# Cross attention on Trainium2: on ScalarE the next unit's exponential ahead of this unit's high half

## The chip, the cores and the metric

The kernel runs on one core of one Trainium2 chip. The metric is the device time of one execution in microseconds (us). Before the change it is 1541.23 us, the median of 3 runs (1541.2 to 1542.07).

## The reference, cut to what matters

The kernel computes a two layer decoder for 8 sequences of 256 tokens with 256 channels: window attention, cross attention, experts, a gated recurrence, a second cross attention and a feed forward part, each with a residual and a layer norm. The change touches only the two cross attentions. What one of them computes (the first masks with an integer mask, the second adds a mask; both have 16 heads of 16 channels and 77 context rows a batch):

```python
Q = proj(query, Wq, bq)
K = proj(key, Wk, bk)
V = proj(value, Wv, bv)
scores = jnp.einsum('bhqd,bhkd->bhqk', Q, K) / np.sqrt(D_K)
scores = jnp.where(m == 0, NEG, scores)
attn = jax.nn.softmax(scores, axis=-1)
x = jnp.einsum('bhqk,bhkd->bhqd', attn, V)
x = x.transpose(0, 2, 1, 3).reshape(b, -1, D_MODEL)
return x @ Wo.T + bo
```

## The kernel before

The stages run one after the other, with a barrier of all engines between them. A cross attention (function `cross_attention`, called twice, tags ca0 and ca1) goes through 8 batches; a batch has 8 units (`UNITS`), numbered c = 0 to 7. A unit is one tile of 128 tokens with 4 of the 16 heads. Each engine runs a queue of its own in the order in which its program is written, and the queues meet only at semaphores. What one unit needs, in the order of the data:

- TensorE `score(b, c)` (L1134): scores of 4 heads, 128 x 308, into one of two PSUM banks.
- VectorE `mask_scores` (L1008 in the second stage, L1010 in the first): masks the scores into `z`. Then `take_maximum` (L1016) writes the maxima of `z` into `top`.
- GpSimd `subtract` (L887): `z` minus the maxima, semaphore `shift`.
- ScalarE `power` (L951): the exponential of `z` into `probs`, semaphore `exped`. Called exp(c) below.
- TensorE `turn_probs` (L1143): transposes the four heads of `probs` into PSUM, semaphore `probs_t`. Called turn(c).
- ScalarE (L959): the high half of the turned probabilities as fp16 into `pth`, semaphore `probs_high`. Called pth(c). It frees nothing by itself: the PSUM bank stays in use until the low half is taken.
- VectorE `probs_rest` (L1021): the low half into `ptl`, semaphore `probs_low`. Called ptl(c). It needs pth(c).
- TensorE `weigh` (L1157): 12 small products of the two halves with the two halves of the values.

`z`, `top`, `probs`, `pth`, `ptl` and the PSUM banks all exist twice, so unit c and unit c + 2 share one.

The loops are staggered by hand. In the pass for unit c:

- TensorE: turn(c), score(c + 2), one step of the projections, weigh(c - 1).
- VectorE: mask(c + 2), ptl(c), top(c + 2), then whatever the unit has besides (normalising, residual and its statistics, the layer norm's last step, values).
- GpSimd: subtract(c + 2), then in some units the masked keys (L881), a token sum (L895) or the root of the variance (L155).
- ScalarE: pth(c), exp(c + 1), then the eviction of the projection step, if it is ScalarE's.

The projection steps come from a planner, the ring `CA`, one a unit: keys (evicted at L937 into `kb`), values, heads (L939, `ot`), mix, tokens (L929, `xt`), query (L932, `q`), heads, mix. They serve the next batch for keys, values, tokens and query, and the one before for the first heads and mix. The first and the last batch leave some out. DMAs are issued from SyncE only: the context and the tokens of the batch after next.

Of the kernel before, what the change touches and what calls it, by code (L numbers as in the profile page):

```python
# [162 lines left out]
def first(b):  # L163

    return isinstance(b, int) and b == 0
# [547 lines left out]
UNITS = TPB * CH // UH  # L713
# [39 lines left out]
def cross_attention(nc, weights, ctx_dram, ident, half, X, next_loads=None):  # L753
    tag, additive = weights.tag, weights.additive
    w, bias, rows, mask = weights.w, weights.bias, weights.rows, weights.mask
    with ExitStack() as ctx:
# [59 lines left out]
        def wait_read(engine, steps, b):  # L816
            CA.wait_read(engine, free, steps, b)
# [6 lines left out]
        def both(batch):  # L824

            def run(engine):
                batch(0, 0, before=False)
                with engine.Fori(0, BATCH // 2 - 1) as i:
                    batch(2 * i + 1, 1)
                    batch(2 * i + 2, 0)  # L830
                batch(BATCH - 1, 1, after=False)
            return run
# [4 lines left out]
        @block.sync  # L837
        def _(sp):
            def load_context(b, par):
                sp.dma_start(context[par][:], ctx_dram[:, :, bass.ds(b * CTX, CTX)]).then_inc(context_loaded[par], 16)  # L840

            def stage(b, par):

                sp.dma_start(xs[par][:], X[:, bass.ds(b * TPB, TPB)]).then_inc(staged[par], 16)

            for b in (0, 1):
                load_context(b, b)
                stage(b, b)
            if next_loads:
                next_loads(sp)  # L850

            def replace(b, par):

                wait_full(sp, "value", 0, b)
                load_context(b + 2, par)
                wait_full(sp, "tokens", 0, b)
                sp.wait_ge(token_sum, (b + 1) * TPB)
                stage(b + 2, par)

            replace(0, 0)  # L860
            replace(1, 1)
            with sp.Fori(1, BATCH // 2 - 1) as i:
                replace(2 * i, 0)
                replace(2 * i + 1, 1)
# [54 lines left out]
        @block.scalar  # L919
        def _(act):  # L920
            act.wait_ge(weights.loaded, 64)

            def step(b, par, kind, i, bank, uses):
                src = shared[bank]
                if kind in ("mix", "value"):
                    return
                act.wait_ge(full[bank], uses + 1)
                if kind == "tokens":
                    ins = act.activation(xt[par][:], src[:].rearrange("p (g q) -> p g q", g=KT_), ACT.Copy)  # L929
                elif kind == "query":  # L930
                    for g in range(KT_):
                        ins = act.activation(q[par][:, g], src[:, g * SEQ:(g + 1) * SEQ], ACT.Identity, bias=bias[:, 0, g:g + 1])  # L932
                elif kind == "key":
                    if not first(b):
                        act.wait_ge(key_masked, b * KT_)
                    for g in range(KT_):
                        ins = act.activation(kb[:, g], src[:, g * CTX:(g + 1) * CTX], ACT.Identity, bias=bias[:, 1, g:g + 1])  # L937
                elif kind == "heads":
                    ins = act.activation(ot[:, i], src[:, 0:DIM].rearrange("p (g q) -> p g q", g=KT_), ACT.Copy)  # L939
                ins.then_inc(free[bank], 1)  # L940

            def value_high(b, par):
                wait_read(act, [("value", 0)], b)
                act.activation(vh[par][0:CTX, :, 0:CD], v[0:CTX], ACT.Copy, scale=SCALE).then_inc(v_high, 1)

            def power(b, c):
                k = c % 2
                act.wait_ge(shift, b * UNITS + c + 1)
                if not (first(b) and c < 2):
                    act.wait_ge(probs_t, b * UNITS + c - 1)  # L950
                act.activation(probs[k][:], z[k][:], ACT.Exp, scale=1.0 if additive else CD ** -0.5).then_inc(exped, 1)  # L951

            def batch(b, par, before=True, after=True):
                for c in range(UNITS):
                    k = c % 2
                    act.wait_ge(probs_t, b * UNITS + c + 1)
                    if not (first(b) and c < 2):
                        act.wait_ge(weighted, b * UNITS + c - 1)
                    act.activation(pth[k][0:CTX], t_bank[k][0:CTX], ACT.Copy, scale=PSCALE).then_inc(probs_high, 1)  # L959
                    if c < UNITS - 1:  # L960
                        power(b, c + 1)
                    elif after:
                        power(b + 1, 0)
                    for kind, i, bank, uses in CA.slot(c, b):
                        d = CA.serves(kind, i)
                        step(b + d, (par + d) % 2, kind, i, bank, uses)
                    if c == 2 and after:
                        value_high(b + 1, 1 - par)

            act.wait_ge(ones, 1)  # L970
            for kind, i, bank, uses in CA.prologue():
                step(0, 0, kind, i, bank, uses)
            value_high(0, 0)
            power(0, 0)
            both(batch)(act)
            for kind, i, bank, uses in CA.epilogue():
                step(BATCH - 1, 1, kind, i, bank, uses)
# [1664 lines left out]
```

## Time and profile before

| | before |
|---|---|
| median of 3 runs | 1541.23 us |
| profiled execution | 1540.88 us, its span 1539.1 us |
| TensorE busy | 1201.4 us (78%) |
| VectorE busy | 1101.3 us (72%) |
| ScalarE busy | 672.9 us (44%) |
| GpSimd busy | 506.7 us (33%) |
| high half of turned probabilities (L959) | 128 instructions, 593 ns each |
| exponentials of the cross attentions (L951) | 128 instructions, 455 ns each |
| low half (L1021) | 128 instructions, 677 ns each |

The first cross attention lies at about 547 to 720 us of the span, the second at about 1271 to 1442. Busy time counts the execution of instructions; an engine that waits for a semaphore is idle, and the profile names what ended the wait. Consecutive instructions of one engine overlap a little, so distances from start to start say more of the pace than durations do. The granted clock is a share of TensorE's full 2.4 GHz: 1.00 is that, 0.50 is 1.2 GHz, values between are a mean over a stretch.

### The profile page before, as it was taken

Reading aid. Unit: us, or ns where it says so; the run is one execution under the profiler, and the core shown is the slowest. Engines: PE = TensorE matmul, PEld = TensorE weight load, DVE = VectorE, ACT = ScalarE, POOL = GpSimd, SP = SyncE. Lnnn points to the kernel's source line nnn. Section 1 sums busy time; section 2 is a strip of 40 time slices with the busy share of each in tenths; the row PEclk is TensorE's granted clock in tenths of the full one; section 3 lists DMA queues with packets and bytes.
Section 4 is the critical chain, followed back from the end, with each engine's and each line's share of the span. In section 5 each row is a group of like instructions: output and inputs, shape, how many; then the busy total and the mean of one; then the engine's idle time right before and its main releaser. Section 6 shows DMA issues by size and latency. Waiting matters only on the chain. (4 is left out here: it accounts for less than half of the span.)

```text
span 1539.1 us, 29853 instructions
## 1 busy us (share of the span) xinstructions
PE 1201.4 (78%) x10299; PEld 988.2 (64%) x10300; DVE 1101.3 (72%) x2315; ACT 672.9 (44%) x1379; POOL 506.7 (33%) x494
## 2 busy tenths in 40 slices
PE   4889888898898869996113566749989957999687
PEld 1577776776777857775113566748878846777576
DVE  5687877777787638886872766646888764888678
ACT  3454544443454325653101333424655523655184
POOL 3212111021110025553723332133453433555323
PEclk8899999998999979997556787969999977999699
DMA  5000000010000000002512332030000002000011
GB/s 187 8 1 9 9 1 10 6 54 3 1 1 1 2 20 20 18 16 86 194 59 95 126 129 86 26 110 17 21 20 10 5 0 79 28 18 7 28 35 48
DMA packets 31079, 61.39 MB, mean 40 GB/s; under 512 B 7610, under 2 KB 20602, under 8 KB 27898
## 3 DMA queue, kind: packets, MB, share of 16 engines
q1 hardware_dynamic: 29434, 55.76, 10.2%
q0 software_dynamic: 1536, 4.20, 0.9%
q8 instruction: 66, 1.08, 0.3%
q14 instruction: 43, 0.35, 0.1%
HBM read 41.13 MB, written 10.42 MB: 33 GB/s over the span
## 5 line engine op out<-in xcount | busy, mean ns | idle before, releaser
L345 POOL TENSOR_TENSOR wa_rot<-wa_raw,wa_cos_sin 128x1024 f32<-128x1024 f32 x32 | 80.5, 2517 | 347.9 <-ACT wa_raw L389 345.6
L887 POOL TENSOR_TENSOR ca_z<-ca_z,ca_top 128x308 f32<-128x308 f32 x128 | 92.6, 724 | 136.8 <-DVE ca_top L1016 136.5
L639 PE MATMUL wa_scores<-wa_kt,wa_qt 128*128 128x192 f32 x512 | 121.8, 351 | 0.0
L2211 PE MATMUL re_g<-re_conv,re_w_g 128*128 128x256 f32 x512 | 112.8, 379 | 0.0
L2211 PEld LDWEIGHTS re_g<-re_conv,re_w_g 128*128 128x128 f32 x512 | 97.3, 190 | 13.2
L959 ACT ACTIVATE ca_pth<-ca_turned 77x512 f16<-77x512 f32 x128 | 75.9, 593 | 61.1 <-PE ca_turned L1143 60.5
L1143 PE MATMUL ca_turned<-ident,ca_probs 128*77 128x128 f32 x512 | 85.2, 290 | 21.1 <-ACT ca_probs L951 20.0
L1134 PE MATMUL ca_scores<-ca_km,ca_q 128*128 128x308 f32 x256 | 90.7, 438 | 6.0 <-ACT ca_q L932 5.7
L605 PE MATMUL wa_shared<-wa_wh,wa_xh 128*128 128x512 f16 x192 | 76.0, 396 | 17.9 <-ACT wa_raw L389 8.9
L1765 PE MATMUL ex_down<-ex_hh,ex_w2h 128*128 128x160 f16 x224 | 53.8, 256 | 45.1 <-DVE ex_hl L1719 45.1
L639 PEld LDWEIGHTS wa_scores<-wa_kt,wa_qt 128*128 128x128 f32 x512 | 80.3, 198 | 13.3 <-issue 1.3
L1021 DVE SCALAR_TENSOR_TENSOR ca_ptl<-ca_turned,ca_pth 77x512 f16<-77x512 f32 x128 | 86.7, 677 | 2.7 <-ACT ca_pth L959 2.7
L526 DVE SCALAR_TENSOR_TENSOR wa_ptl<-wa_turned,wa_pth 128x384 f16<-128x384 f32 x128 | 65.5, 550 | 22.1 <-ACT wa_pth L430 20.7
L389 ACT ACTIVATE wa_raw<-wa_shared 128x512 f32<-128x512 f32 x64 | 38.1, 597 | 97.6 <-PE wa_shared L605 97.6
L468 DVE TENSOR_TENSOR wa_sine<-wa_raw,wa_cos_sin 128x512 f32<-128x512 f32 x64 | 63.6, 1035 | 23.6 <-ACT wa_raw L389 13.9
L503 DVE TENSOR_REDUCE wa_top<-wa_scores 128x2 f32<-128x384 f32 x128 | 70.2, 548 | 10.9 <-PE wa_scores L639 10.6
L951 ACT ACTIVATE ca_probs<-ca_z 128x308 f32<-128x308 f32 x128 | 58.2, 455 | 45.0 <-POOL ca_z L887 44.0
L605 PE MATMUL wa_shared<-wa_wl,wa_xh 128*128 128x512 f16 x192 | 75.5, 393 | 0.0
L605 PE MATMUL wa_shared<-wa_wh,wa_xl 128*128 128x512 f16 x192 | 75.0, 390 | 0.0
L613 PE MATMUL wa_shared<-ident,wa_rot 128*128 128x128 f32 x256 | 41.9, 296 | 42.3 <-DVE wa_vl L480 37.5
L505 DVE TENSOR_TENSOR wa_shifted<-wa_scores,wa_top 128x384 f32<-128x384 f32 x128 | 71.3, 557 | 4.4
L1143 PEld LDWEIGHTS ca_turned<-ident,ca_probs 128*77 128x77 f32 x512 | 56.7, 150 | 26.9 <-ACT ca_probs L951 22.5
(311 smaller groups left out, 3871.7 us busy)
## 6 DMA issues: line engine op xcount, KB each, us to landing
ex_stage<-in_ew SPq DMA_DIRECT2D x16, 1024.0 KB, 6.8
ca_xs<-tokens SPq DMA_DIRECT2D x16, 256.0 KB, 2.4
slots<-rt_zeros SPq DMA_DIRECT2D x4, 920.0 KB
wa_w_stage<-in_wqkv SPq DMA_DIRECT2D x6, 512.0 KB, 4.2
ex_xe<-slots SPq DMA_DIRECT2D x16, 160.0 KB, 2.3
slots<-ex_y SPq DMA_DIRECT2D x15, 160.0 KB
wa_x_stage<-in_xt SPq DMA_DIRECT2D x8, 256.0 KB, 3.0
tokens<-in_x SPq DMA_DIRECT2D x1, 2048.0 KB, 10.2
```

Source lines behind the costliest of these rows:

```text
L345: pool.tensor_tensor(rot[:, r % 2], raw[:, r % 2], c, ALU.mult).then_inc(cos_done, 1)
L503: dve.tensor_reduce(top[:, k], s_bank[t][:, :, 0:SPAN], AX.X, ALU.max).then_inc(maxed, 1)
L505: dve.tensor_tensor(shifted[k][:], s_bank[t][:, :, 0:SPAN], top[:, k].unsqueeze(2).broadcast_to((P, 2, SPAN)), ALU.subtract).then_inc(shif ...
L526: dve.scalar_tensor_tensor(out=windows(ptl[k][:]), in0=windows(t_bank[h][:]), scalar=PSCALE, in1=windows(pth[k][:]), op0=ALU.mult, op1=ALU ...
L605: ins = pe.matmul(dst[:], a[:, par, k, tok], w[:, k, cols], start=(k == 0 and n == 0), stop=(k == KT_ - 1 and n == 2))
L639: ins = pe.matmul(dst, qt[par][:, 2 * u + h, t * P:(t + 1) * P], kt[par][:, u, t * WINDOW:t * WINDOW + SPAN], start=False, stop=True)
L887: pool.tensor_tensor(z[k][:], z[k][:], top[:, k].unsqueeze(2).broadcast_to((P, UH, CTX)), ALU.subtract).then_inc(shift, 1)
L959: act.activation(pth[k][0:CTX], t_bank[k][0:CTX], ACT.Copy, scale=PSCALE).then_inc(probs_high, 1)
L1021: dve.scalar_tensor_tensor(out=ptl[k][0:CTX], in0=t_bank[k][0:CTX], scalar=PSCALE, in1=pth[k][0:CTX], op0=ALU.mult, op1=ALU.subtract).then ...
L1134: pe.matmul(s_bank[c % 2][:, 0:UH * CTX], q[par][:, g, t * P:(t + 1) * P], km[par][:, g, h:h + UH].rearrange("p h k -> p (h k)"), start=Tr ...
L1143: ins = pe.transpose(t_bank[k][0:CTX, h * P:(h + 1) * P], probs[k][:, h], ident[:])
L2211: ins = pe.matmul(g_bank[m][:, k], w_g[:, j, cols], conv[par][:, j], start=(j == 0), stop=(j == HT - 1))
```

## The change

On ScalarE the exponential of unit c + 1 is issued ahead of the high half of unit c, with its waits. The pass for unit c becomes exp(c + 1), pth(c), eviction. Everything else, on ScalarE and on the other engines, stands as it did.

```diff
             def batch(b, par, before=True, after=True):
                 for c in range(UNITS):
                     k = c % 2
+                    if c < UNITS - 1:
+                        power(b, c + 1)
+                    elif after:
+                        power(b + 1, 0)
                     act.wait_ge(probs_t, b * UNITS + c + 1)
                     if not (first(b) and c < 2):
                         act.wait_ge(weighted, b * UNITS + c - 1)
                     act.activation(pth[k][0:CTX], t_bank[k][0:CTX], ACT.Copy, scale=PSCALE).then_inc(probs_high, 1)
-                    if c < UNITS - 1:
-                        power(b, c + 1)
-                    elif after:
-                        power(b + 1, 0)
                     for kind, i, bank, uses in CA.slot(c, b):
```

## Rows read from the trace of the kernel before

**Rows 1.** Window: length, busy of PE, PEld, DVE, ACT, POOL (count), clock, DMA.
```profile
600.00:620.00 20.00, 19.16 (x200) 15.74 (x198) 17.43 (x46) 11.56 (x25) 11.08 (x15) 1.00 0.07 20
```
**Rows 2.** Costliest groups, both stages: busy, mean ns | idle before, releaser.
```profile
L959 ACT ACTIVATE ca_pth<-ca_turned 77x512 f16<-77x512 f32 x128 | 75.9, 593 | 61.1 <-PE ca_turned L1143 60.5
L1143 PE MATMUL ca_turned<-ident,ca_probs 128*77 128x128 f32 x512 | 85.2, 290 | 21.1 <-ACT ca_probs L951 20.0
...
L1021 DVE SCALAR_TENSOR_TENSOR ca_ptl<-ca_turned,ca_pth 77x512 f16<-77x512 f32 x128 | 86.7, 677 | 2.7 <-ACT ca_pth L959 2.7
...
L951 ACT ACTIVATE ca_probs<-ca_z 128x308 f32<-128x308 f32 x128 | 58.2, 455 | 45.0 <-POOL ca_z L887 44.0
```
**Rows 3.** Timelines of VectorE, GpSimd, ScalarE, second stage: start, duration, instruction, idle before.
```profile
1404.94 0.68 DVE L1021 SCALAR_TENSOR_TENSOR ca_ptl<-ca_turned,ca_pth 77x512 f16<-77x512 f32 x1
1405.54 0.46 DVE L1016 TENSOR_REDUCE ca_top<-ca_z 128x4 f32<-128x308 f32 x1
...
1406.08 0.81 POOL L887 TENSOR_TENSOR ca_z<-ca_z,ca_top 128x308 f32<-128x308 f32 x1 [0.43 <-DVE ca_top L1016]
...
1406.92 0.46 ACT L951 ACTIVATE ca_probs<-ca_z 128x308 f32<-128x308 f32 x1 [0.62 <-POOL ca_z L887]
...
1408.63 0.45 ACT L951 ACTIVATE ca_probs<-ca_z 128x308 f32<-128x308 f32 x1
1409.09 0.60 ACT L929 ACTIVATE ca_xt<-ca_shared 128x512 f32<-128x512 f32 x1
...
1410.44 0.70 POOL L887 TENSOR_TENSOR ca_z<-ca_z,ca_top 128x308 f32<-128x308 f32 x1 [0.79 <-DVE ca_top L1016]
...
1411.17 0.46 ACT L951 ACTIVATE ca_probs<-ca_z 128x308 f32<-128x308 f32 x1 [0.71 <-POOL ca_z L887]
...
1430.17 0.59 ACT L959 ACTIVATE ca_pth<-ca_turned 77x512 f16<-77x512 f32 x1 [0.75 <-PE ca_turned L1143]
1430.67 0.45 ACT L951 ACTIVATE ca_probs<-ca_z 128x308 f32<-128x308 f32 x1
1431.02 0.37 ACT L939 ACTIVATE ca_ot<-ca_shared 128x256 f32<-128x256 f32 x1
...
1430.80 0.69 DVE L1021 SCALAR_TENSOR_TENSOR ca_ptl<-ca_turned,ca_pth 77x512 f16<-77x512 f32 x1 [0.28 <-ACT ca_pth L959]
```
**Rows 4.** Timelines again: ptl(1), ptl(62) of stage one, ptl(1), pth(63) of two.
```profile
569.96 0.68 DVE L1021 SCALAR_TENSOR_TENSOR ca_ptl<-ca_turned,ca_pth 77x512 f16<-77x512 f32 x1
...
708.26 0.69 DVE L1021 SCALAR_TENSOR_TENSOR ca_ptl<-ca_turned,ca_pth 77x512 f16<-77x512 f32 x1 [0.28 <-ACT ca_pth L959]
...
1292.84 0.68 DVE L1021 SCALAR_TENSOR_TENSOR ca_ptl<-ca_turned,ca_pth 77x512 f16<-77x512 f32 x1
...
1431.87 0.59 ACT L959 ACTIVATE ca_pth<-ca_turned 77x512 f16<-77x512 f32 x1 [0.48 <-PE ca_turned L1143]
```
**Rows 5.** Timelines again: a query's eviction and the mask behind it; a residual unit.
```profile
615.57 0.84 ACT L932 ACTIVATE ca_q<-ca_shared,ca_bias 128x256 f32<-128x256 f32 x2 [0.49 <-PE ca_shared L1103]
...
618.02 0.48 DVE L1010 TENSOR_TENSOR ca_z<-ca_scores,ca_limit 128x308 f32<-128x308 f32 x1 [1.78 <-PE ca_scores L1134]
618.41 0.68 DVE L1021 SCALAR_TENSOR_TENSOR ca_ptl<-ca_turned,ca_pth 77x512 f16<-77x512 f32 x1
...
1407.24 0.46 DVE L1016 TENSOR_REDUCE ca_top<-ca_z 128x4 f32<-128x308 f32 x1
...
1408.91 0.48 DVE L1008 SCALAR_TENSOR_TENSOR ca_z<-ca_scores,ca_mask 128x308 f32<-128x308 f32 x1
```
**Rows 6.** Windows of 2 us, columns as in rows 1, start and end of stage one.
```profile
566.00:568.00 2.00, 2.00 (x11) 1.88 (x10) 1.45 (x3) 0.29 (x2) 0.11 (x1) 0.50 0.00 0
...
570.00:572.00 2.00, 1.98 (x32) 1.52 (x30) 1.62 (x5) 0.77 (x2) 0.91 (x2) 1.00 0.00 0
...
706.00:708.00 2.00, 0.85 (x6) 0.66 (x7) 1.95 (x6) 0.82 (x2) 1.78 (x4) 1.00 0.00 0
708.00:710.00 2.00, 1.88 (x20) 1.65 (x19) 0.69 (x1) 1.40 (x4) 1.25 (x2) 0.76 0.00 0
```

## Prediction

> **What bounds the kernel now.** I read the windows by stage first, then the page's costliest groups, then the timelines of single engines in order of time. The change touches only the two cross attentions, each of which runs 64 units (8 batches of 8). In the middle of a stage TensorE is busy 19.16 of 20 us at the full clock, VectorE 17.43, ScalarE 11.56, GpSimd 11.08 [rows 1]. So TensorE and VectorE set the pace together, and ScalarE is idle for over 40% of the time. The groups say what ScalarE waits for: ahead of the high halves (L959) 60.5 us for the turned probabilities, ahead of the exponentials (L951) 44.0 us for GpSimd's shifted scores; and TensorE waits 20.0 us for an exponential ahead of the transposes [rows 2]. VectorE's low half (L1021) waits 2.7 us in 128 units for the high half [rows 2]: the high half is hardly ever late now. One unit takes, from the first to the last undisturbed low half (ptl of unit 1 to ptl of unit 62, 61 steps), 708.26 - 569.96 = 138.30 us in the first stage and 1430.80 - 1292.84 = 137.96 us in the second, 2.27 and 2.26 us a unit [rows 3, 4].
>
> **The change part by part.** No instruction is added or removed. One is moved: exp(c+1), with its two waits (shift of unit c+1, turned of unit c-1), stands ahead of pth(c) and its waits. ScalarE issues no DMA here, and no other queue is reordered.
>
> What it gives: exp(c+1) no longer waits for turn(c), so the transposes of unit c+1 can start earlier. The most that this can return is the 20.0 us that TensorE waits for exponentials [rows 2].
>
> What it adds: pth(c) now waits for shift(c+1). Behind it on ScalarE stand the unit's evictions (xt, q, kb, ot) and the next exponential; waiting for it are ptl(c) on VectorE and through that weigh(c) on TensorE. The point is where shift(c+1) comes from. VectorE works in the order mask(c+2), ptl(c), top(c+2) (L1008 or L1010, L1021, L1016), GpSimd subtracts when top is there, and ScalarE takes the exponential when that is done. With the new order this closes a ring:
>
> ptl(c) -> top(c+2) -> subtract(c+2) -> exp(c+2) -> pth(c+1) -> ptl(c+1)
>
> Each turn of this ring goes through every one of its five steps and brings the kernel on by a single unit. In the old order pth(c+1) stood ahead of exp(c+2), so the ring was open. All five links are in the trace as start to start distances:
> - ptl to top: 1405.54 - 1404.94 = 0.60 us [rows 3].
> - top to subtract: 1406.08 - 1405.54 = 0.54 us [rows 3].
> - subtract to an exponential that waits for it: 1406.92 - 1406.08 = 0.84 us at the high end, 1411.17 - 1410.44 = 0.73 us at the low end [rows 3]. The longer ones come where VectorE works on SBUF beside it, in three of eight units as I read the batches; I take 0.77.
> - exp to pth: never seen back to back. The nearest is exp to another eviction of PSUM that stands behind it: 1431.02 - 1430.67 = 0.35 us to ot, 1409.09 - 1408.63 = 0.46 us to xt [rows 3]. xt may have waited for its own transposes, so I take 0.35 and keep 0.46 as the bound.
> - pth to a ptl that waits for it: 1430.80 - 1430.17 = 0.63 us [rows 3].
>
> The ring takes 0.60 + 0.54 + 0.77 + 0.35 + 0.63 = 2.89 us; with the ends 2.85 to 3.07. That is above the 2.27 us of now, so it becomes the bound of every unit.
>
> What is late next must fit beside it. From a mask to the ptl behind it are 618.41 - 618.02 = 0.39 us [rows 5], so VectorE has 2.89 - 0.60 - 0.39 = 1.90 us from a top to the next mask; the unit with a residual and its statistics took 1408.91 - 1407.24 = 1.67 us [rows 5]. Tight but covered. The query step: counting from exp(5), q stands behind pth(5) on ScalarE, which is the last thing it waits for, at 2.89 + 0.35 + 0.50 = 3.74 (0.50 from a pth to what stands behind it, 1430.67 - 1430.17 [rows 3]); from q to the mask of the next batch's first scores was 618.02 - 615.57 = 2.45 us [rows 5], so 6.19, and ptl could start 0.39 later, at 6.58; the ring wants ptl(6) at 2 x 2.89 + 0.35 + 0.63 = 6.76. Covered by 0.18 us; were it not, it costs that overshoot once in a batch, a few us in all. The ring also swallows what now makes the long units: the 20.0 us of TensorE and the waits for q cost nothing any more, and nothing of them is to be subtracted, since the ring is counted whole.
>
> At the front of a stage nothing changes up to ptl(1), which is held by the scores at the low clock. At its end exp(63) to pth(63) takes 1431.87 - 1430.67 = 1.20 us through the transposes, and pth(62) now starts 0.35 after exp(63) instead of 1431.87 - 1430.17 = 1.70 us ahead of pth(63) [rows 3, 4]: 0.85 in place of 1.70, a gain of 0.85 us a stage.
>
> **The sum.** 2 x 61 x 2.89 = 352.6 us in place of 138.30 + 137.96 = 276.3; less 2 x 0.85 = 1.7: +74.6 us. Against the profiled execution's own 1540.88 us (span 1539.1) this is 1615.5; the median, 1541.23, is 0.35 us above it, so 1616 us. With the ring at 2.85 it is 1611, at 3.07 it is 1638.
>
> **Rivals.**
> *The gain that the words promise.* If shift(c+1) were there before the transposes of unit c end, exp(c+1) would fill idle time of ScalarE, pth(c) would not move, and TensorE's 20.0 us would go [rows 2]: 1541 - 20 = 1521 us. It decides from whether subtract(c+1) ends ahead of turned(c) once the units close up. Against it: ScalarE already waits 44.0 us for GpSimd with the exponential standing later [rows 2], so the shift is late in many units before anything is made faster. The Trainium skill (Perfetto Trace Analysis, Optimizing DMA Performance, Optimization Strategies) says: "When the matmul engine is idle waiting for other engines to finish their work, optimize those engines that are blocking the critical path to keep the matmul engine going." By that rule the exponential is the thing to bring forward, and the time is this rival's; the trace does not bear the rule out as far as the engine it feeds takes more from another queue.
>
> *Late without feeding back.* The high halves are late only by what the exponentials wait for GpSimd, 44.0 us in all, and VectorE makes up the rest: 1541 + 44 = 1585 us. For it: VectorE has some idle time. Against: the ring is made of queue order and semaphores alone; no slack enters it.
>
> *The TensorE clock falls.* In a ring of 2.89 us TensorE has about 2.27 x 0.96 = 2.17 us of work a unit [rows 1], and short idle times in each unit. At the end of the first stage, where the units have few steps, it was busy 0.85 and 1.88 us in two stretches of 2 us, and the granted clock went from 1.00 to 0.76, that is from 2.4 to 1.2 GHz within the stretch [rows 6]. At the start of the stage TensorE worked without a pause at 0.50 (566 to 568) and had 1.00 again by 570 [rows 6]. The clock can thus fall in light units and come back in about 5 us. Such a fall takes 2.5 us of TensorE's work; two units have 2 x (2.89 - 2.17) = 1.4 us to spare, so it costs 1 to 2.5 us. One in each of 16 batches: 16 to 40 us, some 1644 us. Against it: most units keep a step and are at 75% or more, and in the steady stretch the clock is 1.00 [rows 1]. The Trainium skill (TensorE: Matmul & The Clock Gate, A second HAM failure mode: psum-queue depth-cycling) has a kernel in which short idle times between groups of matmuls made the clock swing; the fall at 709 agrees with that.
>
> *It does nothing*, because something else orders ScalarE: I see no such thing; 1541 us.
>
> **How the numbers follow.** The ring 0.70 (1616 us), the ring with a falling clock 0.19 (1644), late without feeding back 0.06 (1585), the gain 0.04 (1521), nothing 0.01. The range takes the ring's bounds, 1611 to 1638, a little below for links that are shorter in a calm pipeline, and the clock rival to a little over its middle: 1604 to 1650. Slower by over 0.2% (about what a measurement of this kernel can tell from no change) 0.95, within 0.2% 0.01, faster 0.04.
>
> **What would show it.** Right: in the middle of a stage the starts of ptl lie 2.9 us apart whatever the unit's step; the idle time ahead of L1021 goes from 2.7 us to over 100 us, released by pth on ScalarE; the wait for the turned probabilities ahead of L959 (60.5 us) goes nearly to nothing, and the one ahead of L951 for GpSimd grows from 44.0 to well over 100; TensorE's busy share falls to about three quarters; the stages take 37 us more each and everything outside them the same. Wrong: units still of uneven length (another chain binds), a granted clock under 1 between 575 and 740 (the clock rival), or L1021 hardly waiting (the gain).

## The result

The changed kernel takes 1617.66 us (median of 4 runs, 1615.28 to 1619.52) against 1541.22 us before (1541.12 to 1542.07): ratio 1.051, 95% interval 1.0482 to 1.0537 (the plain quotient of the two medians is 1.0496). It is 76 us slower. The profiled execution took 1615.28 us with a span of 1613.5, 74.4 us over the span before.

The page of the changed kernel: head, and the costliest groups of the cross attentions (busy, mean ns | idle time before, releaser), to be laid beside [rows 2].

```profile
span 1613.5 us, 29853 instructions
...
PE 1221.3 (76%) x10299; PEld 994.1 (62%) x10300; DVE 1108.0 (69%) x2315; ACT 659.4 (41%) x1379; POOL 506.4 (31%) x494
...
L1021 DVE SCALAR_TENSOR_TENSOR ca_ptl<-ca_turned,ca_pth 77x512 f16<-77x512 f32 x128 | 87.8, 686 | 93.9 <-ACT ca_pth L963 92.2
L951 ACT ACTIVATE ca_probs<-ca_z 128x308 f32<-128x308 f32 x128 | 58.8, 460 | 213.0 <-POOL ca_z L887 212.8
L1143 PE MATMUL ca_turned<-ident,ca_probs 128*77 128x128 f32 x512 | 89.3, 300 | 53.3 <-ACT ca_probs L951 52.9
...
L963 ACT ACTIVATE ca_pth<-ca_turned 77x512 f16<-77x512 f32 x128 | 73.6, 575 | 0.7 <-PE ca_turned L1143 0.7
```

The number of instructions is the same and every engine's busy time is nearly so; what grew is waiting. VectorE's low half, which waited 2.7 us for the high half [rows 2], now waits 92.2 us for it. ScalarE's exponential waits 212.8 us for GpSimd in place of 44.0, and its high half, behind it in the queue, only 0.7 us for the transposes in place of 60.5. And TensorE, whose wait for exponentials the new order was to shorten, waits 52.9 us for them in place of 20.0: bringing the exponential forward in ScalarE's queue made it later in time.

One turn of the ring in the first stage: timelines of VectorE, GpSimd and ScalarE, sorted by start.

```profile
653.17 0.69 DVE L1021 SCALAR_TENSOR_TENSOR ca_ptl<-ca_turned,ca_pth 77x512 f16<-77x512 f32 x1 [1.48 <-ACT ca_pth L963]
653.78 0.46 DVE L1016 TENSOR_REDUCE ca_top<-ca_z 128x4 f32<-128x308 f32 x1
...
654.32 0.70 POOL L887 TENSOR_TENSOR ca_z<-ca_z,ca_top 128x308 f32<-128x308 f32 x1 [1.55 <-DVE ca_top L1016]
...
655.05 0.46 ACT L951 ACTIVATE ca_probs<-ca_z 128x308 f32<-128x308 f32 x1 [1.91 <-POOL ca_z L887]
655.42 0.57 ACT L963 ACTIVATE ca_pth<-ca_turned 77x512 f16<-77x512 f32 x1
...
655.46 0.48 DVE L1010 TENSOR_TENSOR ca_z<-ca_scores,ca_limit 128x308 f32<-128x308 f32 x1
656.03 0.69 DVE L1021 SCALAR_TENSOR_TENSOR ca_ptl<-ca_turned,ca_pth 77x512 f16<-77x512 f32 x1
```

Start to start the links are 0.61, 0.54, 0.73, 0.37 and 0.61 us: 2.86 us from one low half to the next. The mask of this unit, the one with the residual, starts at 655.46, 0.57 ahead of the low half: it fitted, as the 1.90 us against 1.67 had it [rows 5]. The next turn, in which the subtraction shares its time with a VectorE instruction on SBUF, has 0.84 in the third place:

```profile
657.17 0.80 POOL L887 TENSOR_TENSOR ca_z<-ca_z,ca_top 128x308 f32<-128x308 f32 x1 [1.10 <-DVE ca_top L1016]
...
658.01 0.46 ACT L951 ACTIVATE ca_probs<-ca_z 128x308 f32<-128x308 f32 x1 [1.59 <-POOL ca_z L887]
...
658.98 0.69 DVE L1021 SCALAR_TENSOR_TENSOR ca_ptl<-ca_turned,ca_pth 77x512 f16<-77x512 f32 x1 [1.18 <-ACT ca_pth L963]
```

The ends of the two stages, to be laid beside [rows 4]: ptl(1) and ptl(62) of stage one, then of stage two, and ptl(63).

```profile
566.10 0.68 DVE L1021 SCALAR_TENSOR_TENSOR ca_ptl<-ca_turned,ca_pth 77x512 f16<-77x512 f32 x1
...
743.13 0.69 DVE L1021 SCALAR_TENSOR_TENSOR ca_ptl<-ca_turned,ca_pth 77x512 f16<-77x512 f32 x1 [0.84 <-ACT ca_pth L963]
...
1326.96 0.68 DVE L1021 SCALAR_TENSOR_TENSOR ca_ptl<-ca_turned,ca_pth 77x512 f16<-77x512 f32 x1
...
1504.16 0.69 DVE L1021 SCALAR_TENSOR_TENSOR ca_ptl<-ca_turned,ca_pth 77x512 f16<-77x512 f32 x1 [0.84 <-ACT ca_pth L963]
1505.03 0.69 DVE L1021 SCALAR_TENSOR_TENSOR ca_ptl<-ca_turned,ca_pth 77x512 f16<-77x512 f32 x1 [0.18 <-ACT ca_pth L963]
```

So the 61 turns took 743.13 - 566.10 = 177.03 us and 1504.16 - 1326.96 = 177.20 us, 2.90 us each on average, where they took 138.30 and 137.96. The 74.4 us of the span come out as: ahead of ptl(1) of stage one -3.9, the 61 turns of stage one +38.7, between there and ptl(1) of stage two -0.8, stage two +39.2, behind it +1.0. The -3.9 is no part of the effect: the first cross attention's first instruction on GpSimd (L868) already starts 4.2 us earlier, at 543.03 in place of 547.21, and what stands ahead of it, the window attention, was not changed.

### The profile page after: what moved, and what is told of

Same layout as the page of the kernel before. It is cut to its first block and busy times, and to the rows that moved or that the text cites. A ratio compares the mean times of both kernels' runs of the same rounds, so it can differ in the third digit from the quotient of the medians.

```text
span 1613.5 us, 29853 instructions
## 1 busy us (share of the span) xinstructions
PE 1221.3 (76%) x10299; PEld 994.1 (62%) x10300; DVE 1108.0 (69%) x2315; ACT 659.4 (41%) x1379; POOL 506.4 (31%) x494
## 5 line engine op out<-in xcount | busy, mean ns | idle before, releaser
L1021 DVE SCALAR_TENSOR_TENSOR ca_ptl<-ca_turned,ca_pth 77x512 f16<-77x512 f32 x128 | 87.8, 686 | 93.9 <-ACT ca_pth L963 92.2
L951 ACT ACTIVATE ca_probs<-ca_z 128x308 f32<-128x308 f32 x128 | 58.8, 460 | 213.0 <-POOL ca_z L887 212.8
L1143 PE MATMUL ca_turned<-ident,ca_probs 128*77 128x128 f32 x512 | 89.3, 300 | 53.3 <-ACT ca_probs L951 52.9
L1134 PE MATMUL ca_scores<-ca_km,ca_q 128*128 128x308 f32 x256 | 95.6, 458 | 8.4 <-ACT ca_q L932 8.4
```

Source lines behind the costliest of these rows:

```text
L1021: dve.scalar_tensor_tensor(out=ptl[k][0:CTX], in0=t_bank[k][0:CTX], scalar=PSCALE, in1=pth[k][0:CTX], op0=ALU.mult, op1=ALU.subtract).then ...
L1134: pe.matmul(s_bank[c % 2][:, 0:UH * CTX], q[par][:, g, t * P:(t + 1) * P], km[par][:, g, h:h + UH].rearrange("p h k -> p (h k)"), start=Tr ...
L1143: ins = pe.transpose(t_bank[k][0:CTX, h * P:(h + 1) * P], probs[k][:, h], ident[:])
```

## The experiments

Each was timed against the kernel before on the same chip; that one's medians were 1538.39 us in the first set of four, 1539.03 in the second, 1534.81 in the last two. What follows is read by the ratio, or by the difference to the kernel before of its own set.

**The ring cut at VectorE, ScalarE's order left new.** In the changed kernel:

```diff
                     if two_on:
                         mask_scores(*two_on)
-                    probs_rest(b, c)
                     if two_on:
                         take_maximum(*two_on)
+                    probs_rest(b, c)
```

> The changed kernel with one thing more: VectorE takes the maxima of unit c + 2 ahead of the low half of unit c, straight behind its mask. The ring theory: ptl(c) no longer stands ahead of top(c + 2), so the ring of five links is cut, with ScalarE's order left as the change made it. What is left is VectorE's own work, about 1.98 us a unit plus 0.1 for a maximum that stands straight behind its mask (0.51 us from mask to top at the stage's front against 0.39 to a ptl), some 2.1 us a unit: 1520 to 1545 us, and the idle time ahead of the low half falls from 94 us to under 25. The rival, that the exponential ahead of the high half costs by itself (ScalarE's queue held by GpSimd): stays at 1600 to 1617 us.

It took 1561.59 us, ratio 1.014 (1.0097 to 1.0183), +23 us in place of +76. The low half waits 13.1 us. With ScalarE left alone, one moved call on VectorE took away over two thirds of the loss, so the new order does not cost that by itself. But it is 17 us above what I expected at most, and that remained to be explained.

**The same move in the kernel before.**

> The kernel before with the same move on VectorE alone, the control for the last one. Ring theory: there was no ring to cut; the loop over two units (exponential, transposes, scores, mask, maximum, subtraction) loses the low half, about 0.5 us in two units, and VectorE gains 0.1 us a unit of its own work: 1520 to 1545 us. If it is within 5 us of the last one, ScalarE's order is worth next to nothing once the ring is cut; if the last one is faster by 10 us or more, the words of the change hold a real gain that the ring hid.

1546.74 us, ratio 1.0052 (1.003 to 1.0073): +8 us, just outside the 1520 to 1545 that I gave. The maximum ahead of the low half is no gain in itself, and ScalarE's new order still costs 15 us on top of it: bringing the exponential forward holds no gain that the ring hid.

**New order in every second pass.** The block of `power` stands ahead of the high half only where the condition holds, `c % 2 == 0` in one kernel and `c % 2 == 1` in the other; elsewhere it stands behind, as in the kernel before. `next_power` is a local function around that block. The diff is against the changed kernel, cut:

```diff
-                    if c < UNITS - 1:
-                        power(b, c + 1)
-                    elif after:
-                        power(b + 1, 0)
+                    if c % 2 == 1:
+                        next_power()
                     act.wait_ge(probs_t, b * UNITS + c + 1)
...
+                    if not (c % 2 == 1):
+                        next_power()
```

> The exponential ahead of the high half in the even passes only (c = 0, 2, 4, 6), the old order in the odd ones. Ring theory: the ring needs two neighbouring passes in the new order, so it is open here; in the trace before, the exponentials of the even passes were the ones that did not wait for GpSimd (they stood queued behind pth), so little moves: 1530 to 1550 us. The rival, a cost per moved exponential: half of the 76 us, 1579 us.

> The same in the odd passes only (c = 1, 3, 5, 7), whose exponentials waited for GpSimd before (44.0 us in 56 of them). Ring theory: open again, but every second high half now waits for the shift and a loop over two units is closed: exp, pth, ptl, then mask, ptl, top, subtraction, 0.35 + 0.63 + 1.4 + 0.60 + 0.54 + 0.77 = 4.3 us for two units, 2.15 a unit, just under the 2.27 of now: 1541 to 1570 us, slower than the even passes. The rival, a cost per moved exponential: 1579 us, the same as for the even passes.

Even passes: 1546.02 us, ratio 1.0051 (1.0032 to 1.0071), +8 us. Odd passes: 1597.11 us, ratio 1.0381 (1.035 to 1.0412), +59 us. The same number of exponentials is moved in both, and the odd passes cost over seven times as much as the even ones: there is no price per moved exponential. But the odd passes are far outside the 1541 to 1570 that I gave. Their timeline shows why: from the low half of one odd pass to that of the next.

```profile
654.54 0.69 DVE L1026 SCALAR_TENSOR_TENSOR ca_ptl<-ca_turned,ca_pth 77x512 f16<-77x512 f32 x1 [1.18 <-ACT ca_pth L966]
655.15 0.46 DVE L1021 TENSOR_REDUCE ca_top<-ca_z 128x4 f32<-128x308 f32 x1
655.53 0.24 DVE L1033 RECIPROCAL ca_inv<-ca_out 128x16 f32<-128x16 f32 x1
655.81 0.42 DVE L1037 TENSOR_TENSOR ca_o<-ca_out,ca_inv 128x256 f32<-128x256 f32 x1
656.15 0.41 DVE L996 TENSOR_TENSOR ca_v<-ca_shared,ca_rows 77x256 f32<-77x256 f32 x1
656.48 0.47 DVE L1015 TENSOR_TENSOR ca_z<-ca_scores,ca_limit 128x308 f32<-128x308 f32 x1
656.86 0.68 DVE L1026 SCALAR_TENSOR_TENSOR ca_ptl<-ca_turned,ca_pth 77x512 f16<-77x512 f32 x1
657.46 0.46 DVE L1021 TENSOR_REDUCE ca_top<-ca_z 128x4 f32<-128x308 f32 x1
...
658.00 0.81 POOL L887 TENSOR_TENSOR ca_z<-ca_z,ca_top 128x308 f32<-128x308 f32 x1 [0.43 <-DVE ca_top L1021]
...
658.84 0.46 ACT L951 ACTIVATE ca_probs<-ca_z 128x308 f32<-128x308 f32 x1 [1.38 <-POOL ca_z L887]
659.21 0.57 ACT L966 ACTIVATE ca_pth<-ca_turned 77x512 f16<-77x512 f32 x1
...
659.82 0.69 DVE L1026 SCALAR_TENSOR_TENSOR ca_ptl<-ca_turned,ca_pth 77x512 f16<-77x512 f32 x1 [1.18 <-ACT ca_pth L966]
```

One new order pass is enough for a loop, over two units: VectorE goes without a pause from 654.54 to 657.46 through all of its work of a unit and a half, then the same subtraction, exponential and high half follow, 5.28 us in all, 2.64 a unit. My 4.3 us had left out VectorE's other work between a maximum and the next mask: 0.95 us here (L1033, L1037, L996: 655.53 to 656.48), up to 1.29 with a residual. The heavy units of VectorE are the odd ones (c = 1, 3, 5, 7). In the even passes there is at most 0.33 us of it, by which I estimate the loop at 4.3 to 4.6 us, 2.15 to 2.3 a unit, about the 2.27 of now; that goes with +8.

**Both moves in every second pass**, to try that reading; nothing else differs from the two kernels above than VectorE's maximum ahead of the low half.

> New order in the odd passes only, and VectorE takes the maximum ahead of the low half. My reading of the odd passes run (1597 us, outside what I expected) is a loop over two units: low half, maximum, VectorE's other work of the pass, mask, next low half, next maximum, subtraction, exponential, high half: 5.3 to 5.5 us. With the maximum ahead of the low half, one maximum and one low half leave it: 0.60 + 0.95 to 1.29 (other work) + 0.51 + 0.54 + 0.77 + 0.37 = 3.7 to 4.1 and the 0.6 to the low half, 4.3 to 4.7 us for two units. The same loop would be what holds the run with the new order in all passes and the maximum ahead (1561.6 us). So it should fall from 1597 to within 6 us of that: 1555 to 1567 us. If VectorE's own work has no part in the loop, the odd passes stay above 1580.

> New order in the even passes only, and the maximum ahead. In the even passes VectorE has 0 to 0.33 us of other work, so the two unit loop is 3.4 to 3.8 us, 1.9 a unit, well under VectorE's own 2.1: nothing of ScalarE's order is left, and it should be that of the old order with the maximum ahead, 1546.7 us: 1541 to 1552 us. If a swapped pass costs something of its own once the loops are short, it lies half way to 1561.6, 1554.

Odd: 1560.08 us, ratio 1.0169 (1.0125 to 1.0212). Even: 1545.22 us, ratio 1.006 (1.0038 to 1.0083). Both lie where I expected them from the two unit loop: with one maximum and one low half out of it the odd passes fall from +59 to +25 us, the same as with all passes swapped (+23), and the even ones stand with the old order (+10 and +8). So the rest of the first experiment, 15 us over its control, sits in the odd passes. The low halves wait 13.1 and 10.3 us for high halves in the two kernels with odd passes swapped, 2.5 and 3.0 in the two without. That is most of the 15 us; how the rest is made up is not shown.

**A longer link, in both orders.** On GpSimd, ahead of the subtraction of every unit, an addition whose result nobody reads, with its own semaphore:

```diff
                 pool.wait_ge(maxed, b * UNITS + c + 1)
+                pool.tensor_tensor(spare[:, 0:SPARE], rows[:, 1, 0:SPARE], rows[:, 0, 0:SPARE], ALU.add).then_inc(spared, 1)
+                pool.wait_ge(spared, b * UNITS + c + 1)
                 k = c % 2
```

> The changed kernel with one link made longer: GpSimd adds two tiles of 128 x 128 in between the maximum and the subtraction of every unit (a result that nobody reads), and the subtraction waits for it. From its 128 x 256 additions (0.72 to 0.79 us) and 128 x 308 subtractions (0.70) I estimate 0.4 to 0.5 us for it with its semaphore. Ring theory: every unit pays it in full, 122 turns of the ring: 49 to 61 us over the changed kernel, 1665 to 1678 us, and the low halves lie 3.3 to 3.4 us apart. The rival, that the changed kernel is bound by something else (VectorE, TensorE at a lower clock) and GpSimd has idle time to take it: within 15 us of 1617.

> The same addition in the kernel before. Ring theory: with the high half ahead of the exponential the subtraction lies in a loop over two units only (exponential, transposes, scores, mask, low half, maximum, subtraction), so it costs at most half a link a unit, 61 x 0.45 x 2 / 2 = 27 us, and less where other waits cover it: 1541 to 1570 us, at most half of what it costs in the new order. The rival, that GpSimd's work counts the same in both orders: the same 49 to 61 us.

In the new order 1679.28 us (ratio 1.0921, 1.0885 to 1.0957), 140.3 us over the kernel before of its set, where the changed kernel stands 76.4 over its own: the addition costs 64 us, and the time is 1 us above the 1665 to 1678 that I gave. The low halves lie 3.42 us apart, in both stages, in place of 2.90. GpSimd's timeline in the new order:

```profile
652.49 0.45 POOL L889 TENSOR_TENSOR ca_spare<-ca_rows 128x128 f32<-128x128 f32 x1 [2.15 <-DVE ca_top L1021]
653.02 0.70 POOL L892 TENSOR_TENSOR ca_z<-ca_z,ca_top 128x308 f32<-128x308 f32 x1
```

It takes 0.53 us from its start to that of the subtraction, and 122 x 0.53 = 64.7 us: the turns pay it all but in full (3.42 - 2.90 = 0.52 us), though GpSimd had stood idle for 2.15 us ahead of it. In the old order the same instruction costs 1563.74 - 1539.03 = 24.7 us (ratio 1.0159, 1.0124 to 1.0194), 0.20 us a unit: under half.

**New order in the first stage only**, with `if not additive` as the condition (`additive` is true in the second one, which adds its mask).

> The new order in the first cross attention only. If the loss is made inside each stage by its 61 turns of the ring, it is half: 38 us, 1576 to 1580 us, with the second stage's low halves 2.26 us apart as before. If one stage carries the loss (a clock that falls, the table load at the second stage's front), it is near 1541 or 1617.

1577.98 us, ratio 1.0259 (1.0226 to 1.0291), +39 us of 76. The low halves wait 48.3 us for high halves, half of 92.2; they lie 2.90 us apart in the first stage and 2.26 in the second. Each stage makes its own half of the loss.

**New order in pass 6 only**, `c == 6`.

> The exponential ahead of the high half in pass 6 only. There GpSimd's shift is early (616.07 us against an exponential at 616.84 in the trace before) and the low half waits for the mask anyway, and VectorE has nothing besides in that pass. If the price lies in loops and not in the moved instruction, it costs nothing: 1536 to 1545 us, with the kernel before between 1534 and 1543. The rival, a price per moved exponential (76 us for 128): 16 of them, 9.5 us over the kernel before.

1538.82 us, ratio 1.0005 (0.9984 to 1.0026): no difference. The interval reaches from 2.5 us faster to 4 us slower, so a price of 9.5 us is excluded and a gain of up to 2.5 us is not. No kernel that I ran is shown to be faster than the one before.

## Why the prediction was right

I had 1616 us, from 1604 to 1650; it is 1617.66.

*The ring.* Forecast 0.60 + 0.54 + 0.77 + 0.35 + 0.63 = 2.89 us, measured 2.90 us a unit as a mean over 61 units in both stages. Its one unseen link, exp to pth, for which I had taken the 0.35 of another eviction against 0.46, is 0.37; pth to ptl is 0.61 in place of 0.63. The third link is 0.73 in one of the turns shown and 0.84 in the next, the two ends that I had read. The stages grew by 38.7 + 39.2 = 78.0 us, forecast 352.6 - 276.3 = 76.3.

Not every unit goes by the ring. In each stage 58 of the 61 distances are 2.84 to 2.97 us, 2.89 on average, and three are longer. Two are 3.23 to 3.27 us, at ptl(24) and ptl(40), the first unit of a turn of the program's loop over pairs of batches, where VectorE stands still for about 0.6 us ahead of the mask. The third is ptl(60), 3.02 us in stage one and 3.16 in stage two, where the mask waits for scores at the low clock. VectorE's timelines of stage one:

```profile
632.52 0.48 DVE L1010 TENSOR_TENSOR ca_z<-ca_scores,ca_limit 128x308 f32<-128x308 f32 x1 [0.60 <-ACT ca_probs L951]
632.92 0.68 DVE L1021 SCALAR_TENSOR_TENSOR ca_ptl<-ca_turned,ca_pth 77x512 f16<-77x512 f32 x1
...
737.04 0.48 DVE L1010 TENSOR_TENSOR ca_z<-ca_scores,ca_limit 128x308 f32<-128x308 f32 x1 [0.35 <-PE ca_scores L1134]
737.44 0.68 DVE L1021 SCALAR_TENSOR_TENSOR ca_ptl<-ca_turned,ca_pth 77x512 f16<-77x512 f32 x1
```

The prediction's sum has neither; they make up the 1.7 us between 76.3 and 78.0. The releaser that the first line names cannot be the real one, since the exponential that this mask needs had ended over 3 us before; that it is the loop's turn is read from the place alone, and no run tries it.

*The ends.* From ptl(62) to ptl(63) 1505.03 - 1504.16 = 0.87 us, forecast 0.85, where it had been 1.69; in stage one 0.89 in place of 1.82. Behind ptl(62) of the second stage the span is 1.0 us longer all the same. TensorE's granted clock was at 0.50 for the last products of the stage, where it had been 1.00 before. The four products of the last but one mix (L1123) took twice as long, and VectorE waited for them. Before:

```profile
1431.67 1.03 PE L1123 MATMUL ca_shared<-ca_w,ca_ot 128*128 128x256 f32 x4
```

Changed:

```profile
1504.55 2.04 PE L1123 MATMUL ca_shared<-ca_w,ca_ot 128*128 128x256 f32 x4 [0.18 <-ACT ca_ot L939]
...
1506.63 0.42 DVE L1038 TENSOR_TENSOR ca_res<-ca_shared,ca_xb 128x256 f32<-128x256 f32 x1 [0.92 <-PE ca_shared L1123]
```

That uses up the gain at this end: from ptl(62) to the stage's last L159 are 10.88 us in place of 10.69. The other 0.8 us of the 1.0 lie behind the stage, in code that was not changed.

*Luck.* That the profiled execution, 1615.28 us, comes within 0.3 us of the forecast 1615.5 is luck: the 61 turns were 1.7 us longer than forecast, the gain at the second end and 0.8 us more were lost behind it, and the window attention happened to be 4.2 us shorter. What the prediction is right about is the ring and its length to 0.01 us a unit.

*What was to fit beside the ring* did: the residual unit is shown above. For the query step, forecast with 0.18 us to spare, the timelines of ScalarE and VectorE:

```profile
670.38 0.82 ACT L932 ACTIVATE ca_q<-ca_shared,ca_bias 128x256 f32<-128x256 f32 x2
...
672.57 0.48 DVE L1010 TENSOR_TENSOR ca_z<-ca_scores,ca_limit 128x308 f32<-128x308 f32 x1
673.36 0.69 DVE L1021 SCALAR_TENSOR_TENSOR ca_ptl<-ca_turned,ca_pth 77x512 f16<-77x512 f32 x1 [0.32 <-ACT ca_pth L963]
```

The mask was there, and it was the high half that the low half waited for, 0.32 us. The step from q to mask took 2.19 us, not the 2.45 that I had [rows 5].

*The rivals.* The gain needs an exponential that TensorE gets earlier; it got them later. The loss without feeding back (1585 us) fell with the ring's 2.89 us in 58 of 61 units and with the added link that nearly every turn pays. The clock rival had its event right, six times in place of sixteen, and its price wrong; a granted clock under 1 inside the stages, which the prediction had named as a sign of being wrong, did come. Windows of 2 us of the changed kernel (length, busy of PE, PEld, DVE, ACT, POOL, clock):

```profile
634.00:636.00 2.00, 0.98 (x18) 0.88 (x17) 0.82 (x3) 0.94 (x2) 0.80 (x1) 1.00 0.00 0
636.00:638.00 2.00, 0.87 (x5) 0.38 (x4) 1.86 (x6) 0.26 (x1) 0.99 (x2) 0.84 0.00 0
638.00:640.00 2.00, 2.00 (x20) 1.76 (x20) 1.65 (x4) 1.26 (x4) 1.03 (x2) 0.50 0.00 0
640.00:642.00 2.00, 2.00 (x20) 1.62 (x19) 0.92 (x3) 0.94 (x2) 0.68 (x1) 0.80 0.00 0
```

```profile
635.86 0.69 DVE L1021 SCALAR_TENSOR_TENSOR ca_ptl<-ca_turned,ca_pth 77x512 f16<-77x512 f32 x1 [1.18 <-ACT ca_pth L963]
...
638.72 0.69 DVE L1021 SCALAR_TENSOR_TENSOR ca_ptl<-ca_turned,ca_pth 77x512 f16<-77x512 f32 x1 [0.35 <-ACT ca_pth L963]
...
641.68 0.69 DVE L1021 SCALAR_TENSOR_TENSOR ca_ptl<-ca_turned,ca_pth 77x512 f16<-77x512 f32 x1 [0.46 <-ACT ca_pth L963]
```

TensorE was idle for about half of 4 us, and then worked at 1.2 GHz until 641. The low halves kept their distance, 2.86 and 2.96 us, and each waited for the high half, not for TensorE. Such falls come at about 637, 661 and 730 in stage one and 1399, 1423 and 1491 in stage two. I had charged each 1 to 2.5 us, taking TensorE's lost work less its idle share; but what counts is how far its results are ahead of the ring, and in this fall they were still ahead of the high half. Only the third fall of each stage reached the ring, with 3.02 - 2.85 = 0.17 us and 3.16 - 2.86 = 0.30 us at ptl(60), as shown above; a further fall, at the end of stage two, took away the gain there.

*Where a reading of mine failed* was not in the prediction but in what I expected of the odd passes: I took a loop's length from the links between engines and left out what stands between two of its instructions in VectorE's own queue. It did not matter in the ring of one unit, since nothing stands between ptl(c) and top(c + 2).

*Marks that I had named.* The low half was to wait over 100 us and waits 92.2; the prediction has no sum for the 100. In many units VectorE gets from its other work and the mask to the low half without an idle time, as in the residual unit above. The wait for the turned probabilities was to go nearly to nothing and is 0.7 us, and the exponentials' was to be well over 100 us and is 212.8. The starts of the low halves were to lie 2.9 us apart, and but for three units a stage they do. TensorE's busy share was to fall to three quarters: 15.59 us of 20 in the window from 600 to 620, against 19.16 [rows 1].

## What to carry to other kernels

When two instructions of one queue are swapped, follow what the earlier one waits for around all queues: if that leads back to the later one, a ring is closed, and its length is the sum of all its links, however idle the engines in it are. Here five links of 0.37 to 0.84 us, with ScalarE and GpSimd idle for over half of the time (8.35 and 8.62 us busy of 20 in the window from 600 to 620), set the pace at 2.90 us where the kernel before takes 2.27. A ring can be opened at a link other than the one that closed it: moving VectorE's maximum ahead of the low half gave back 53 of 76 us, though the best order stayed the one in which the high half never waits for the next unit.

When such a loop spans two passes, count also what each engine has to do between the two instructions that belong to the loop; here that was 0.95 us out of 5.28.

## What was not expected of the hardware

- At 637 us the granted clock fell from 2.4 to 1.2 GHz. Ahead of the fall TensorE was busy 0.98 and 0.87 us in two windows of 2 us; its two longest idle times there were 1.02 and 1.13 us, with work before, between and after. The Trainium skill (TensorE: Matmul & The Clock Gate, A second HAM failure mode: psum-queue depth-cycling) tells of a clock that swings with short idle times between groups of matmuls; these windows agree with it. The same share of work does not always go with a fall: from 1442 to 1446 us TensorE was busy 1.11 and 0.87 us in two such windows, and the clock stayed at 1.00. The falls cost 0 to 0.3 us each while the ring set the pace, and about 1 us at the end of stage two.
- In each of the four kernels with the maximum ahead of the low half 13 subtractions on GpSimd take 1.21 to 1.40 us in place of 0.70 to 0.81, about one in a batch. Every one of them overlaps VectorE's last step of the layer norm (L159), which itself takes 0.93 us in place of 0.40 in most of these cases. In the first of the four:

```profile
641.90 1.22 POOL L887 TENSOR_TENSOR ca_z<-ca_z,ca_top 128x308 f32<-128x308 f32 x1 [0.45 <-DVE ca_top L1016]
...
642.34 0.93 DVE L159 TENSOR_SCALAR tokens<-ca_res,ca_mv,ca_rstd 128x256 f32 x1
```

  Overlap alone does not do it: in the changed kernel a subtraction at 625.01 us, with L159 starting 0.47 us behind it, takes 0.70 us and L159 0.41. What does is open. Thirteen subtractions at about 0.5 us each are 7 us, near the 8 us that the move costs in the old order, but that they are its cause is only argued.
- The same kernels show six idle times of VectorE, 0.29 to 0.61 us, whose releaser is "issue". They stand ahead of a mask, three in a stage, at the first units of the turns of the program's loop over pairs of batches, where two of the long turns of the changed kernel stand as well.
